# 288 record scatters moved into the gathers of the first aggregation

## The reference

```python
# layer 1: attention, the "first aggregation"
a = leaky_relu(sum((h[src] + edge_attr @ We.T + be) * attn), 0.01)   # edge scores
a = exp(a - segment_max(a, dst)[dst]); a = a / (segment_sum(a, dst)[dst] + 1e-16)
x = x + relu(segment_sum(h[src] * a, dst))
# layer 2: 8 experts, top 2;  layer 3: segment_sum(w * h[dst_as_column], src_as_row), batch norm
# layer 4: gate of the last experts
h = xn @ W_gat                       # 16 columns
e = leaky_relu(a_src[src] + a_dst[dst], 0.2)       # softmax over the edges of a node
scores = layernorm(segment_sum(h[src] * softmax(e), dst) + b_gat).mean(over heads)
out = sum over top-2 experts of weight * (gelu(xn @ W1[e] + b1[e]) @ W2[e] + b2[e])
```

## Time and profile before

| What | Value |
| --- | --- |
| Median of 3 runs | 3983.19 us |
| The profiled execution | 3978.59 us |
| Its span, first to last instruction | 3976.6 us |
| PE busy | 2652.6 us (67%) |
| DVE busy | 1509.7 us (38%) |
| POOL busy | 1882.4 us (47%) |
| Edge scores, first product to last read | 404 to 670 us |
| First aggregation, first to last gather | 677 to 1483 us |

### The profile page before, as it was taken

How to read it: one execution, slowest core, us unless ns; L and a number is a source line. 1 busy time by engine, 2 the same in 40 slices (tenths; PEclk the granted TensorE clock), 3 DMA queues, 4 the chain that set the end, 5 groups by cost and what they waited for, 6 DMA issues and landing times. The chain is left out here.

```text
span 3976.6 us, 46896 instructions
## 1 busy us (share of the span) xinstructions
PE 2652.6 (67%) x10550; PEld 1812.6 (46%) x10551; DVE 1509.7 (38%) x3668; ACT 759.2 (19%) x2605; POOL 1882.4 (47%) x1926
## 2 busy tenths in 40 slices
PE   3259886566666661389999999577776663989810
PEld 2135776333333330266676777333333343666600
DVE  5864112656666548622222222322222224001075
ACT  0136000232222220122222222111111111222200
POOL 0000664556565650056666666166666620666602
PEclk9555555666666665589999999766666665999955
DMA  2012442222232330010000000133333311111001
GB/s 71 26 44 65 149 160 104 69 76 79 75 80 75 80 76 13 0 32 11 12 12 12 12 13 1 60 90 89 91 89 91 90 44 26 18 14 19 8 36 35
DMA packets 125070, 213.67 MB, mean 54 GB/s; under 512 B 56130, under 2 KB 83095, under 8 KB 122711
## 3 DMA queue, kind: packets, MB, share of 16 engines
q0 software_dynamic: 75808, 125.28, 12.8%
q1 hardware_dynamic: 49206, 87.79, 6.5%
HBM read 197.42 MB, written 15.52 MB: 54 GB/s over the span
## 5 line engine op out<-in xcount | busy, mean ns | idle before, releaser
L503 POOL DMA_INDIRECT a0rows<-table,a0idx x462 | 472.4, 1022 | 349.6 <-ACT a0idx L488 235.3
L967 POOL DMA_INDIRECT records<-k_recg x288 | 287.4, 998 | 724.5 <-ACTq L306 366.6
L503 POOL DMA_INDIRECT a1rows<-table,a1idx x444 | 420.4, 947 | 316.8 <-ACT a1idx L488 172.1
L533 PE MATMUL a1ps<-a1rows,a1w 128*128 128x256 f32 x888 | 414.0, 590 | 195.3 <-DMA a1rows<-table,a1idx 135.3
L533 PE MATMUL a0ps<-a0rows,a0w 128*128 128x257 f32 x924 | 437.5, 614 | 154.2 <-ACT a0w L703 93.0
L967 POOL DMA_INDIRECT erecords<-k_rece x416 | 404.3, 972 | 209.0 <-issue 98.1
L795 PE MATMUL f0up<-k_xnT,f0w 128*128 x1280 | 380.3, 453 | 54.4 <-ACT f0hid L827 30.6
L1396 POOL DMA_INDIRECT gt_land<-table_gat,gt_source x281 | 266.0, 947 | 293.5 <-DVEq L1425 144.1
L533 PEld LDWEIGHTS a0ps<-a0rows,a0w 128*128 128x128 f32 x924 | 239.0, 292 | 348.5 <-issue 161.9
L533 PEld LDWEIGHTS a1ps<-a1rows,a1w 128*128 128x128 f32 x888 | 209.1, 274 | 400.2 <-issue 283.9
L805 PE MATMUL f0dn<-f0w,f0hid 128*128 128x256 f32 x1600 | 357.8, 380 | 11.4 <-issue 10.7
(11 more groups left out here) (389 smaller groups left out, 3115.2 us busy)
## 6 DMA issues: line engine op xcount, KB each, us to landing
es_ea<-in_eaT SPq DMA_DIRECT2D x16, 1664.0 KB
es_lane<-lane_row SPq DMA_DIRECT2D x16, 832.0 KB
so_rowl<-glane_row SPq DMA_DIRECT2D x32, 256.0 KB
a0rows<-table,a0idx POOLq DMA_INDIRECT x462
a1rows<-table,a1idx POOLq DMA_INDIRECT x444
erecords<-k_rece POOLq DMA_INDIRECT x416
table<-k_tbl SPq DMA_DIRECT2D x10, 650.0 KB, 3.4
records<-k_recg POOLq DMA_INDIRECT x288
```

What stands on the lines that cost most here:

```text
L503: pool.indirect_dma_start(rows[:, i, 0:TW], None, table, bass.IndirectOffsetOnAxis(ap=idx[:, i:i + 1], axis=0)).then_inc(gathered[i], 16)
L533: nc.tensor.matmul(sum_of(t), w[:, i, :], rows[:, i, 0:width], start=False, stop=False).then_inc(agg_done, 1)
L967: pool.indirect_dma_start(self.rec_dram, bass.IndirectOffsetOnAxis(ap=self.rec[:, c + 1, 0:1], axis=0), self.rec[:, c + 1, 1:R], None).the ...
```

## The change

`emit_edge_scores` issues no scatters any more. `emit_aggregate` takes a `Scatter`; only the first aggregation gets one, with all 288 columns. The first 70 blocks (`FULL` = 416/6 rounded up) of POOL's gathers are written out instead of looped, and `share` = 288/70 rounded up = 5: a scatter stands behind each of the first five gathers of a block until all 288 are issued. So the first 57 blocks have five each, the 58th has three, and the others none. The remaining 7 of the 77 blocks run in the loop. SP waits for the scatters and loads the records back inside the first aggregation. The first experts keep the 416 `erecords` scatters alone, spread over the same events of PE.

```diff
-EARLY = 176
+FULL = -(-NC // BG)
@@ emit_edge_scores
-            scatter.finish(sp)
-
-        @block.gpsimd
-        def _(pool):
-            issued = itertools.count()
-            STEPS = 2 * PIECE - 1
-
-            def pace(pool):
-                steps = next(issued) * NPIECE * STEPS // (scatter.last - scatter.first)
-                if steps > STEPS:
-                    pool.wait_ge(step, steps - STEPS)
-
-            scatter.run(pool, pace)
@@ emit_aggregate, POOL
-            pool.reg_mov(count, 0)
-            with pool.Fori(0, total) as g:
+            full = 0
+            if scatter is not None:
+                full, issued = FULL, 0
+                share = -(-(scatter.last - scatter.first) // full)
+                for g in range(full):
+                    for i in range(BG):
+                        pool.wait_ge(indexed, g * BG + i + 1)
+                        pool.indirect_dma_start(rows[:, i, 0:TW], None, table,
+                                                bass.IndirectOffsetOnAxis(ap=idx[:, i:i + 1], axis=0)).then_inc(gathered[i], 16)
+                        if i < share and issued < scatter.last - scatter.first:
+                            scatter.put_one(pool, scatter.first + issued)
+                            issued += 1
+            pool.reg_mov(count, full * BG)
+            with pool.Fori(full, total) as g:
...
+        if scatter is not None:
+            @block.sync
+            def _(sp):
+                scatter.finish(sp)
@@ Scatter
+    def put_one(self, pool, c):
         R = self.rec.shape[2]
-        for c in range(self.first, self.last):
-            turn, lane = divmod(c - self.first, 8)
-            if turn:
-                pool.wait_ge(self.put[lane], 16 * turn)
-            pace(pool)
-            pool.indirect_dma_start(self.rec_dram, bass.IndirectOffsetOnAxis(ap=self.rec[:, c + 1, 0:1], axis=0),
-                                    self.rec[:, c + 1, 1:R], None).then_inc(self.put[lane], 16)
+        turn, lane = divmod(c - self.first, 8)
+        if turn:
+            pool.wait_ge(self.put[lane], 16 * turn)
+        pool.indirect_dma_start(self.rec_dram, bass.IndirectOffsetOnAxis(ap=self.rec[:, c + 1, 0:1], axis=0),
+                                self.rec[:, c + 1, 1:R], None).then_inc(self.put[lane], 16)
@@ build_kernel
-            emit_edge_scores(nc, S, A, Scatter(nc, S, "sa", recg, rec_dram, 0, EARLY))
-        emit_aggregate(nc, S, "a0", table, True)
+            emit_edge_scores(nc, S, A)
+        emit_aggregate(nc, S, "a0", table, True, Scatter(nc, S, "sb", recg, rec_dram, 0, GREC, S.rec_sb))
-            beside = (Scatter(nc, S, "sb", recg, rec_dram, EARLY, GREC, S.rec_sb),
-                      Scatter(nc, S, "sc", rece, erec_dram, 0, NC, S.erec_sb))
+            beside = (Scatter(nc, S, "sc", rece, erec_dram, 0, NC, S.erec_sb),)
```

More of the change, by code:

```diff
@@ L296, in _, with emit_edge_scores @@
                              start=True, stop=True).then_inc(small, 1)
-def emit_edge_scores(nc, S, A, scatter):
+def emit_edge_scores(nc, S, A):
     sem = S.sem
@@ L414, in slot_of, with emit_aggregate @@
                                        "whole blocks of all tiles are at most so many"))
-def emit_aggregate(nc, S, tag, table, softmax):
+def emit_aggregate(nc, S, tag, table, softmax, scatter=None):
     sem = S.sem
@@ L959, in run @@
     def run(self, pool, pace):
+        for c in range(self.first, self.last):
+            pace(pool)
+            self.put_one(pool, c)
+    def put_one(self, pool, c):
         R = self.rec.shape[2]
-        for c in range(self.first, self.last):
-            turn, lane = divmod(c - self.first, 8)
-            if turn:
-                pool.wait_ge(self.put[lane], 16 * turn)
-            pace(pool)
-            pool.indirect_dma_start(self.rec_dram, bass.IndirectOffsetOnAxis(ap=self.rec[:, c + 1, 0:1], axis=0),
-                                    self.rec[:, c + 1, 1:R], None).then_inc(self.put[lane], 16)
+        turn, lane = divmod(c - self.first, 8)
[3 more added lines that the diff above has]
+                                self.rec[:, c + 1, 1:R], None).then_inc(self.put[lane], 16)
     def finish(self, sp):
```

## The result

The kernel after takes 4248.53 us (median of 4 runs, 4233.45 to 4270.18), the kernel before 3983.47 beside it (4 runs): a ratio of 1.067 [1.0622, 1.0718], slower by 265 us. The profiled execution took 4244.72 us, its span 4242.7. The forecast was 4212 with a range to 4260, so number and sign stood. Its parts did not.

What follows compares the result with a forecast made beforehand. No engine was full, DVE setting the aggregation's pace; POOL would become its bound. Aggregation +236, edge scores -5 and experts -2 gave +229 us: 4207.6 profiled, forecast 4212 us as a time of runs, range 4155 to 4260.

Steps and rivals of the forecast that it cites:

- POOL's beat: First aggregation: eleven DMAs a block at 1.255 us plus collisions make POOL the bound, 14.5 us instead of 10.17.
- the 0.7 us for collisions: First aggregation: time per block that POOL's DMAs lose beside DVE's wide mask operations, 0.46 us before the change.
- So the waits of the earlier trace go: First aggregation: POOL's waits for index copies, 218.1 us, vanish under the longer blocks, all but the first of 25.62 us.
- DVE's 23.6 us against PE's 43.5: First aggregation: DVE needs 23.6 us from a tile's finish to the next masks, while PE has three blocks, 43.5 us.
- First rival: First aggregation: waits for indices stay, each of 288 scatters adds its whole 1.26 us, +363, 4339 us in all; chance 0.06.
- the observation that was to prove me wrong: First aggregation: POOL still waiting 3 us at each tile's start in the first 57 blocks would show the waits stay.
- Second rival: First aggregation: DVE's two-input operations wait out POOL's DMAs, 53.7 us a tile, +412, 4388 us in all; chance 0.03.
- Edge scores, −5: Edge scores: 176 scatters less give back 5 us of PE's 35.7 us idle, with ends 0 and -36.
- The first piece says that scatters alone make no gaps: Edge scores: 74 products ran in one go beside scatters without a load, so most of 35.7 us belongs to loads.
- The falsifier: Edge scores: shrinking by over 20 us would show that the scatters and not the loads made PE's gaps.
- First experts, −2: First experts: 112 scatters less remove POOL's backlog at the end, so a load starts earlier, -2 us, ends 0 and -3.
- the same kind of DMA, only thinner: First experts: scatters remain beside PE, 416 instead of 528, so no gain in the stage's body.

Runs made afterwards that it cites:

- e9_looped: Kernel after with POOL looping over the aggregation's blocks, five scatters each always to columns 0 to 4, sorted records zeros; 3927.59 us against 3619.86 for the kernel before.
- e12_halves: Kernel after with 29 scatter blocks written out, 29 looped, small gathers beside edge scores, old pace in experts, records zeros; 3935.72 us, 1.0872 of before.
- e8_spread: Kernel after with the 288 scatters moved: 98 ranking, 38 layer norm, 80 experts, 40 next projection, 32 batch norm; 4026.02 us, 1.0116 of before.
- e5_before: The kernel before, unedited, profiled again on chip 10; 3981.26 us, where the median of the kernel before is 3984.86.
- e6_after: The kernel after, unedited, run again on chip 10; 4246.04 us, 1.0665 of the kernel before.
- e7_after: The kernel after, unedited, run again on chip 6; 4239.23 us, 1.0653 of the kernel before.
- the spreads: Two versions of the kernel after that compute everything, scatters moved out of the aggregation to other stages; 3655.23 us (1.0087 of before) and 4026.02 us (1.0116).
- e1_none: Kernel after without any of the 288 record scatters, zeros standing in for the sorted records; 3624.02 us against 3625.21 for the kernel before.

## Why the prediction was right, and where it was not

- **POOL's beat, 14.5 us a block with five scatters (ends 13.8 and 14.8): right.** Blocks that don't wait mostly take 14.1 to 14.3 us in after, and all of them average 14.3 in `e9_looped` and `e12_halves`. The parts of the sum shifted a little: a DMA took 1.28 us with its gap and not 1.255 (gather and scatter together 2.57), so eleven make 14.1, and of the 0.7 us for collisions next to nothing came; the mean gather even fell from 1022 to 990 ns.
- **"So the waits of the earlier trace rows go": the step that failed.** The sum of DVE's 23.6 us against PE's 43.5 took DVE's durations and gaps from before, as if they belonged to DVE. The durations do. The gaps grew by 355 us over the two scan operations once POOL's DMAs came without a pause, because register instructions between them took 0.70 us. The slack that was to hide DVE's way was used up in each tile, and the third block went from 14.5 to 18 to 31 us. Price: +407 instead of +236. On chips 3 and 9 the same step is right: +315 over a stage of 690, and in `e9_looped` POOL doesn't wait for an index once from the second block's start to the last scatter.
- **First rival, the waits stay: its sign came in part, its reason not.** POOL did wait 13.6 us at tiles' starts, the observation that was to prove me wrong. But no scatter delays a gather beyond its own time; the waits come round through DVE.
- **Second rival, DVE later still: nearest in effect, wrong in mechanism.** A tile took some 55 us in the last part of the stage and some 48 before that, where it had forecast 53.7. It had single operations grow by a DMA of POOL; none did (where six run in a row they take 1.90 us, and mean times are 351 and 348 ns). What grew is the time between instructions, and a register instruction has no tile to read or write, so a lock on memory doesn't explain it. And the mask at line 602, a TENSOR_SCALAR, is hit harder than the operation with two tensor inputs at line 619.
- **Edge scores, −5 with an end at −36: missed, −54.** "The first piece says that scatters alone make no gaps" rested on one piece of 16. The falsifier was named, over 20 us, and came: with the loads unchanged and the scatters gone, the gaps are 0.0. The end of the range was too tight as well, since 10.3 us more came out of busy time and 6.4 from gaps of the float32 products, which I had not counted. On chips 3 and 9 neither scatters nor small gathers make gaps.
- **First experts, −2: missed, −78.** I took "the same kind of DMA, only thinner" for no gain, though the earlier trace rows showed PE with 7 to 9% idle, which I left without a cause. With 416 DMAs instead of 528 PE is gapless at 693 us; 496 gave 733 in `e8_spread`. Of what came back, 50 us were gaps ahead of its two products (54.4 and 11.4 us before, 16.0 and 0.0 after) and 27 us their busy time. The cost there isn't even: 112 scatters more cost 78 us, the first 416 perhaps nothing. The end, where the forecast −2 lay, gave 6: from the last product to the next projection's first it is 12 us instead of 18, counted in "all the rest".
- **Total.** The aggregation came 171 us dearer than forecast, the edge scores 49 and the experts 76 cheaper, the rest some 8 cheaper: 229 + 171 − 49 − 76 − 8 = +267, for +266 measured. 4212 was near 4248 by luck: what dense DMAs of POOL do to the other engines was left out of all three terms, and it counts once against the kernel after (171 us) and twice for it (125). The range held by the same luck; with the aggregation alone as measured and the other two as forecast the time would have been some 4383.

What is shown: where the time lies; that POOL's scatters and not the loads make the gaps of the edge scores on the slower kind of chip, since the loads stayed; that there, and only there, register instructions of DVE and ACT take 0.70 us now and then in the aggregation, that this more than triples with the scatters (96 to 332 on DVE; 94 and 87 in `e5_before` and `e8_spread`, 332 and 302 in `e6_after` and `e7_after`), and that it stops within 5 us when POOL pauses. Inferred only: that dense indirect DMAs hold back the supply of instructions to the other engines. It fits that instructions without operands in memory are hit. Against its simplest form speaks that the profile's `instruction` queues move no more in after than in before (56 packets each). Nine of after's and three of before's fall into the aggregation, of 0.3 to 0.6 us, for over 600 slow instructions in after. Not settled: how POOL's DMAs reach another engine's sequencer; what holds PE in the edge scores and the experts, where no register instruction is slow; what sets the two kinds of chips apart; whether small gathers cost PE as scatters do, and scatters in a loop as written-out ones, on the slower kind; and what turns the long blocks from 19 to 27 us in mid-stage. No version that ran beats both kernels: the spreads are 0.9 and 1.2% behind before.

## What to carry to other kernels

Gaps put down to "issue" on an engine are not its fixed property: ask what else ran densely beside them, and where it now goes, before using an engine's pace as a bound. When background work moves, reckon its cost where it leaves as well as where it arrives; idle time of the host engine that no row explains is what can come back, and busy rows of many instructions can hide more, as 10.3 of the 54 us here. And before comparing two runs, run the kernel before on the same chip.

## What the hardware showed that I had not expected

- The same kernel takes 3620 to 3625 us on two chips and 3976 to 3985 on three others, with single instructions of the engines equally long, loads landing after equal times (6.4 us for `es_ea` in after and in `e9_looped`) and packets of the gathers as long (167 ns in mean in before, 166 in `e1_none`). `e1_none` on the faster kind and before on the slower differ in the stages beside which before issues indirect DMAs: edge scores 212 and 266, aggregation 690 and 805, first experts 693 and 771, second aggregation 607 and 659, last experts 348 and 405. The ranking (118 us) and the projection behind it (46) are equal. These are different kernels, but the differences add up to 357 of the 358 us between the times of before itself.
- A scatter's price on the slower kind depends on its host, in us each: 0.31 in the edge scores (54 for 176), 0.7 in the experts (78 for 112; 0.5 for the 80 of `e8_spread`), 0.74 in the ranking, 0.9 in the projections, 1.4 in the aggregation (407 for 288). On the faster kind it was 0 in the first two and 1.1 (315 for 288) in the aggregation.
- A gather of 260 floats a partition and a scatter of one cost POOL the same, 0.97 and 0.99 us with 0.30 behind: it is paid by the instruction.
- Register instructions of DVE and ACT, some 0.04 to 0.1 us long as a rule, take 0.70 us now and then on the slower kind beside POOL's indirect DMAs: 332 of 1716 and 281 of 1625 in the aggregation of after. On the faster kind none takes over 0.28 us.
